# Both causal masks of a batch ahead of all its score products

## The chip, the cores and the metric

The kernel runs on one core of one Trainium2 chip. The metric is the device time of the whole program in microseconds (us), the median of the timed runs.

## The reference, cut to what matters

Sixteen batches of 112 tokens with 256 features first pass a cross attention with a context of 375 rows (only the start of the kernel). Then come four layers, each with a causal attention of 16 query heads over 4 key heads (64 wide, rotary positions) and a mixture of eight experts of which each token takes two:

```python
q = q * c + _rot_half(q) * sn
k = k * c + _rot_half(k) * sn
scores = jnp.einsum('bhqd,bhkd->bhqk', q, k) / sqrt(HD)
attn = jax.nn.softmax(scores + causal_bias, axis=-1)
out = jnp.einsum('bhqk,bhkd->bhqd', attn, v)
x = clip(res + out @ wo)          # then x = clip(res + moe(rms(x)))
```

## The kernel before

Each engine has its own instruction list, written by hand, and waits on semaphores. A layer's attention goes through the 16 batches one after another; I call one pass of `iteration(b)` **turn b**. Two batches (a pair, g = b // 2) share the projections: five blocks of heads, m = 0 (the keys) to 4 (the queries). TensorE computes a block (`heads_of`, L816), VectorE (DVE) turns it by the rotary tables (`rotate`: L1601, L1603, L1605, signal `d_rope`), and GpSimd (POOL) adds the two parts of blocks 1 to 4 (`add_rotated`, L591, signal `g_rope`). Pair g+1 is projected and rotated while pair g attends: block 0 and 1 in the even turn, blocks 2, 3, 4 in the odd turn, the last ones just before the next turn begins.

The 16 heads of a batch are two halves, p = 0 and p = 1. `scores(l, b, p)` writes one half into two banks of PSUM: p = 0 into banks 0 and 1, p = 1 into banks 2 and 3 (for b > 0). It first writes the causal mask with four small bf16 matmuls (L841), then adds the products of queries and keys (L846, 16 instructions in the trace), and signals `p_sc`. All run on two halves of 64 rows of the array at once. The same banks hold the projected blocks while they are rotated: in odd turns block 0 of the next pair (rotated in the turn before) lies in bank 1 and block 1 in bank 2; before an even turn, blocks 2, 3, 4 lie in banks 0, 1, 2. So the mask of a half may only be written when the rotation of what lay there is over: a wait on `d_rope`, by place. The products of half 0 need `g_rope` of block 2, those of half 1 that of block 4.

After the scores, DVE takes the maxima of each half (`maxima`, L1621, L1622), ScalarE (ACT) eight exponents of each half (L1273, an ACTIVATE and a read of the accumulator each, signal `a_exp`), DVE scales them (L1630, L1631). TensorE meanwhile projects the outputs of the batch before (`out_project`, L896). Behind that it starts the next block, which needs a bank of half 0 back, and therefore waits for the eight exponents of half 0: L816 in odd turns, L824 (the values) in even turns. Then come transposes of the probabilities (L861), more blocks, and the weighing (`weigh`, L872), with which a turn ends. In turns 10 to 13, DVE and POOL also rank the first nine batches' tokens and scatter them to memory (L623) for the experts; turn 15 (b = 15) waits for the first tile of these. Turn 0 of a layer has its scores computed in the layer before.

Of the kernel before, what the change touches and what calls it, by code (L numbers as in the profile page):

```python
# [13 lines left out]
B, S, D = 16, 112, 256  # L14
# [7 lines left out]
GN = GB * S  # L22
# [4 lines left out]
LOADS = 5  # L27
# [87 lines left out]
def xattn_ffn(nc, x, ctx_1024, w_sim, b_sim, W_qv, b_qv, ln1_w, ln2_w, wq, wk, wv, wo, wr, wg, wu, wd, const, out):  # L115
    with ExitStack() as stack:
        def sb(name, shape, dt=F32):
            return stack.enter_context(nc.sbuf_tensor(name, shape, dt))

        def sem(name):  # L120
            return stack.enter_context(nc.semaphore(name))
# [54 lines left out]
        qT = [q.rearrange("p (n t) -> p n t", n=8) for q in q_flat]  # L176
# [29 lines left out]
        rows_b = sb("rows_b", [128, 2, S], BF16)  # L206
        causal_b = sb("causal_b", [128, 2, S], BF16)
# [15 lines left out]
        def route_part(width):  # L223
# [35 lines left out]
        ps = stack.enter_context(nc.psum_tensor("ps", [128, 8, 512], F32))  # L259
# [29 lines left out]
        d_rope, d_max, d_norm, d_wo, d_lg, d_x, d_yr, d_oh, d_rt, d_pos, d_te, d_out, d_gate = (sem(n) for n in (  # L289
            "d_rope", "d_max", "d_norm", "d_wo", "d_lg", "d_x", "d_yr", "d_oh", "d_rt", "d_pos", "d_te", "d_out", "d_gate"))  # L290
# [17 lines left out]
        def bc(ap, axis, shape):  # L308
            return ap.unsqueeze(axis).to_broadcast(shape)
# [5 lines left out]
        def score_bank(b, p):  # L315

            return 2 * p if b else 2 - 2 * p
# [402 lines left out]
        def _(pe):  # L720
# [99 lines left out]
            def values(l, g, bank):  # L820

                for u in range(2):
                    for k in range(KD):
                        last = pe.matmul(ps[0:S, bank, u * D:u * D + NKV * HD], xnT[:, g % 2, k, u * S:u * S + S],  # L824
                                         wv_s[:, k, :], start=(k == 0), stop=(k == KD - 1))
                last.then_inc(p_v, 1)

            def scores(l, b, p):

                g, u = b // 2, b % 2  # L830
                if p == 0:
                    pe.wait_ge(d_rope, l * 40 + g * LOADS + 1)
                pe.wait_ge(g_rope, l * 32 + g * 4 + 2 * p + 2)

                def out(j):
                    return ps[0:S, score_bank(b, p) + j, 0:GN].rearrange("q (h k) -> q h k", h=4)

                for part, k0, k1 in ((0, 0, 64), (1, 64, S)):
                    for j in range(2):
                        js = slice(64 * j, 64 * j + 64)  # L840
                        pe.matmul(out(j)[:, :, k0:k1], causal_b[js, part, :], bc(rows_b[js, part, k0:k1], 1, [64, 4, k1 - k0]),  # L841
                                  start=(part == 0), stop=False)
                for i in range(4):
                    for j in range(2):
                        js = slice(64 * j, 64 * j + 64)
                        last = pe.matmul(out(j)[:, i, :], qT[g % 2][js, 4 * p + i, u * S:u * S + S],  # L846
                                         keys[g % 2][js, p, u * S:u * S + S], start=False, stop=(i == 3))
                last.then_inc(p_sc, 1)

            def layer(l, last_layer):  # L850

# [40 lines left out]
                def out_project(b, p):  # L892

                    pe.wait_ge(a_ot, l * 32 + 2 * b + p + 1)
                    for i in range(4):
                        last = pe.matmul(ps[0:S, 6, 0:D], oT[:, p, i * S:i * S + S], wo_s[:, 4 * p + i, :],  # L896
                                         start=(p == 0 and i == 0), stop=(p == 1 and i == 3))
                    if p:
                        last.then_inc(p_wo, 1)
# [60 lines left out]
                def expert_of(T):  # L960
                    return pe.value_load(tile_e[0:1, bass.ds(T, 1)], min_val=0, max_val=E - 1)
# [25 lines left out]
                def iteration(b):  # L987
                    g, odd = b // 2, b % 2
                    more = g + 1 < NP
                    if b:  # L990

                        if odd and more and b > 1:
                            pe.wait_ge(d_rope, l * 40 + (g + 1) * LOADS + 1)
                        if not odd:
                            pe.wait_ge(d_rope, l * 40 + g * LOADS + LOADS - 1)
                        if b == B - 1:
                            pe.wait_ge(m_xT, l * NT + 2)
                        scores(l, b, 0)
                        if b == B - 2:
                            out_project(b - 1, 0)  # L1000

                        if odd and more:
                            pe.wait_ge(d_rope, l * 40 + (g + 1) * LOADS + 2)
                        if b == RANK_STEP + 1:
                            pe.wait_ge(d_rt, l * NPART + 1)
                        if b == MID_STEP + 1:
                            pe.wait_ge(d_rt, l * NPART + 2)
                        scores(l, b, 1)
                        if b == 1:
                            pe.wait_ge(ld_wo, (l + 1) * 16 * 4)  # L1010
                        if b == B - 1:
                            pe.wait_ge(ld_mw, (l + 1) * 16 * 3 * E)
                            pe.wait_ge(d_te, l * 2 + 1)
                            e0, e1 = expert_of(0), expert_of(1)
                        if b != B - 2:
                            out_project(b - 1, 0)
                        out_project(b - 1, 1)

                    if b == 0:
                        pe.wait_ge(ld_wv, (l + 1) * 16)  # L1020
                        values(l, 0, 7)
                        pe.wait_ge(a_exp, l * 32 + 1)
                        pe.wait_ge(a_t1, l * B + 4)
                        heads_of(l, 1, 0, 2)
                    else:
                        pe.wait_ge(a_exp, l * 32 + 2 * b + 1)
                        if not odd:
                            values(l, g, 0)
                        elif more:
                            heads_of(l, g + 1, 2, 0)  # L1030
                        else:
                            up(0, 0, e0, wg_s, 0, m_g)
                    turn_probs(b, 0)
                    turn_probs(b, 1)
                    if b:
                        turn_x(b - 1)

                    if more:
                        if not odd:
                            pe.wait_ge(a_exp, l * 32 + 2 * b + 1)  # L1040
                            pe.wait_ge(a_t1, l * B + 2 * (g + 1) + 2)
                        heads_of(l, g + 1, 3 if odd else 0 if b else 1, 1 if b else 3)
                    elif odd:
                        up(0, 0, e0, wu_s, 1, m_u)
                    if b == MID_STEP:
                        pe.wait_ge(a_exp, l * 32 + 2 * b + 2)
                        count_rows(1, 3)
                    turn_probs(b, 2)
                    turn_probs(b, 3)
                    if b:  # L1050
                        route_logits(b - 1)

                    if more:
                        pe.wait_ge(a_exp, l * 32 + 2 * b + 2)
                        if b:
                            heads_of(l, g + 1, 4 if odd else 1, 2)
                    else:
                        pe.wait_ge(a_exp, l * 32 + 2 * b + 2)
                        if odd:
                            up(1, 1, e1, wg_s, 2, m_g)  # L1060
                    if b == RANK_STEP:
                        count_rows(0, 3)
                    if b == B - 2:
                        for T in range(2):
                            turn_tile(T, T, 1, 1, T * KD * SLOT)
                    if b == 0:
                        pe.wait_ge(moe_done, l + 1)
                    if not odd:
                        pe.wait_ge(a_v, l * NP + g + 1)
                    if odd and g + 2 < NP:  # L1070

                        pe.wait_ge(a_pt, l * 64 + b * 4 + 3)
                        for k in range(KD):
                            norm_turn(l, g + 2, k, 4, k * TN)
                    weigh(b)

                def tile(T, u, n, first=False, early=False, end=False, count=False):
# [23 lines left out]
                    if early and end:  # L1101
                        pe.wait_ge(m_h, l * NT + NT - 1)
                        scores(l + 1, 0, 0)
# [11 lines left out]
                for b in range(B):  # L1115
                    iteration(b)
# [971 lines left out]
```

## Time and profile before

| what | value |
|---|---|
| median of 3 runs | 1933.63 us (1933.07 to 1934.76) |
| profiled execution, from the first to the last instruction (span) | 1893.5 us |
| PE (TensorE matmul) busy | 1842.4 us, 97% |
| DVE / ACT / POOL busy | 1281.0 / 949.9 / 543.2 us |
| granted TensorE clock, mean | 0.994 |

The profile gives the span as the profiled execution's own time; the median of the runs lies 40.1 us above it, which is what lies before the first and behind the last instruction, and what no instruction of the kernel changes. PE's busy time is partly modelled, so 97% does not say that no wait matters. Below, PEld is TensorE's weight load and PE its matmul; each row of a timeline is start, duration, engine, line, operation, tiles and shapes, count, and in brackets the idle time just before it and what ended that.

### The profile page before, as it was taken

To read this page: it belongs to the slowest core of one execution; us is meant where nothing else is said; L and a number is where in the kernel's file an instruction comes from. 1 tells how busy PE (TensorE), PEld (TensorE's weight loads), DVE (VectorE), ACT (ScalarE), POOL (GpSimd) and SP (SyncE) were. 2 spreads that over 40 slices of the span, in tenths; PEclk is the share of its full clock that TensorE was granted. 3 is DMA by queue.
4 is the path that set the end of the run, shared out by engine and by line. 5 is a ranking of instruction groups with operands and counts; after the bars stand their busy time and mean duration, and the time that the engine had idled before them with its cause. 6 is when DMAs were issued, how large, how long until landed. Compare 5 with 4: busy or idle time off the path is not lost.

```text
span 1893.5 us, 36659 instructions
## 1 busy us (share of the span) xinstructions
PE 1842.4 (97%) x10612; PEld 1359.5 (72%) x10613; DVE 1281.0 (68%) x3173; ACT 949.9 (50%) x3625; POOL 543.2 (29%) x721
## 2 busy tenths in 40 slices
PE   7999999999999999999999999999999999999995
PEld 5887888766668888756667888766667888866663
DVE  4677778754467888764467888764466888855456
ACT  4647776622226777732225777642224777642221
POOL 4752113430022332540032332531031332520014
PEclk9999999999999999999999999999999999999998
DMA  6423220255653330245663340236663331136666
GB/s 165 130 71 107 101 101 6 85 139 143 154 149 102 116 115 7 85 122 142 145 157 89 118 130 27 85 94 147 145 164 93 128 116 44 43 92 149 147 163 172
DMA packets 255292, 212.37 MB, mean 112 GB/s; under 512 B 145826, under 2 KB 226420, under 8 KB 255028
## 3 DMA queue, kind: packets, MB, share of 16 engines
q1 hardware_dynamic: 240808, 174.74, 33.8%
q0 software_dynamic: 13952, 35.33, 6.3%
q8 instruction: 82, 1.34, 0.3%
q14 instruction: 70, 0.57, 0.1%
q10 hardware_dynamic: 380, 0.38, 0.1%
HBM read 137.32 MB, written 73.05 MB: 111 GB/s over the span
## 4 chain that ended last, share of the span: by engine, by line
PE 71%; DVE 9%; ACT 8%; issue 4%; POOL 4%; DMA 3%; SPq 1%; POOLq 0%; DVEq 0%; ACTq 0%
PE ps L930 24%; PE ps L956 12%; ACT parena L1273 8%; PE ps L816 7%; PE ps L896 6%; PE ps L872 4%; PE ps L846 3%; PE ps L861 3%; PE ps L824 3%; POOL qk L591 2%; DVE rope L1601 2%; PE ps L798 2%; PE ps L924 2%; DVE rmax L1621 2%; DVE rope L1605 2%
## 5 line engine op out<-in xcount | busy, mean ns | idle before, releaser
L930 PE MATMUL ps<-arena,xeT 128*128 x1120 | 509.5, 593 | 0.0
L1273 ACT ACTIVATE parena<-ps,nmax 112x112 f32<-112x112 f32 x1024 | 345.6, 387 | 95.3 <-DVE nmax L1622 95.3
L930 PEld LDWEIGHTS ps<-arena,xeT 128*128 128x128 f32 x1120 | 210.1, 190 | 193.5 <-issue 187.3
L591 POOL TENSOR_TENSOR qk<-qk,rope 128x448 f32<-128x448 f32 x128 | 146.3, 1143 | 548.9 <-DVE rope L1605 548.7
L1322 ACT ACTIVATE parena<-ps,er 128x512 f32<-128x512 f32 x140 | 96.2, 687 | 377.1 <-PE ps L930 377.1
L816 PE MATMUL ps<-xnT,wqk_s 128*128 128x224 f32 x1280 | 273.5, 357 | 0.0
L570 POOL DMA_INDIRECT y_in<-sorted_y,pos x114 | 111.2, 975 | 500.6 <-DMA sorted_y<-tarena 397.0
L1273 ACT ACTIVATION_READ_ACCUMULATOR parena<-ps,nmax 112x1 f32 x1024 | 245.9, 240 | 0.0
L896 PE MATMUL ps<-wo_s,oT 128*112 128x256 f32 x1024 | 237.9, 385 | 1.4 <-issue 1.4
L816 PEld LDWEIGHTS ps<-xnT,wqk_s 128*128 128x128 f32 x1280 | 233.5, 191 | 3.1
L1898 DVE SCALAR_TENSOR_TENSOR parena<-parena,ps 128x512 f32<-128x512 f32 x140 | 96.0, 686 | 181.5 <-ACT parena L1322 181.4
L896 PEld LDWEIGHTS ps<-wo_s,oT 128*112 128x112 f32 x1024 | 175.7, 177 | 43.1 <-issue 2.1
L623 POOL DMA_INDIRECT sorted_x<-x_sb,pos_x x128 | 126.8, 991 | 181.6 <-DVE pos_x L1825 147.9
L1621 DVE TENSOR_REDUCE rmax<-ps 112x8 f32<-112x896 f32 x128 | 139.0, 1086 | 56.9 <-PE ps L846 56.8
L1312 ACT ACTIVATE xeT<-ps,ln2T 128x128 f32<-128x128 f32 x280 | 87.4, 365 | 171.8 <-PE ps L924 167.7
L956 PE MATMUL ps<-arena,tarena 128*128 x640 | 153.2, 382 | 2.5 <-issue 1.8
L1282 ACT ACTIVATE tarena<-ps 112x448 f32<-112x448 f32 x256 | 130.2, 583 | 34.4 <-PE ps L861 33.8
L1631 DVE TENSOR_TENSOR parena<-parena,rrec 112x896 f32<-112x896 f32 x128 | 139.8, 1092 | 4.4
L1900 DVE SCALAR_TENSOR_TENSOR parena<-parena,er,ps 128x512 f32<-128x512 f32 x140 | 104.6, 747 | 54.6 <-PE ps L930 54.1
L1286 ACT ACTIVATE oT<-ps 128x448 f32<-128x448 f32 x128 | 69.5, 545 | 131.4 <-PE ps L872 131.4
L956 PEld LDWEIGHTS ps<-arena,tarena 128*128 128x128 f32 x640 | 119.1, 195 | 15.5 <-issue 4.5
L846 PE MATMUL ps<-qk 64*112 64x112 f32 x2048 | 123.4, 260 | 0.0
(207 smaller groups left out, 2785.2 us busy)
## 6 DMA issues: line engine op xcount, KB each, us to landing
sorted_y<-tarena SPq DMA_DIRECT2D x140, 128.0 KB
xe<-sorted_x SPq DMA_DIRECT2D x132, 130.0 KB, 2.5
arena<-in_L_ffn_wg_dram SPq DMA_DIRECT2D x32, 512.0 KB, 3.7
arena<-in_L_ffn_wu_dram SPq DMA_DIRECT2D x32, 512.0 KB, 4.6
arena<-in_L_ffn_wd_dram SPq DMA_DIRECT2D x32, 512.0 KB, 5.6
hid_d<-tarena SPq DMA_DIRECT2D x240, 64.0 KB
tarena<-hid_d SPq DMA_DIRECT2D x60, 256.0 KB, 2.8
hid_d<-parena SPq DMA_DIRECT2D x240, 64.0 KB
```

What stands on the lines that cost most here:

```text
L570: pool.indirect_dma_start(out=y_in[:, b % 2, k, :], out_offset=None, in_=sorted_y[0:FIRST * SLOT, :] if b < PARTS[0][1] else sorted_y, in_ ...
L591: pool.tensor_tensor(q, q, rope[m % 2][:, :], ALU.add).then_inc(g_rope, 1)
L623: pool.indirect_dma_start(out=sorted_x if h == 0 else sorted_x[0:HROWS - WHOLE * SLOT, :], out_offset=bass.IndirectOffsetOnAxis(ap=pos_x[: ...
L816: last = pe.matmul(ps[:, bank, x * TN:x * TN + TN], wqk_s[:, k, n, :], xnT[:, g % 2, k, :], start=(k == 0), stop=(k == KD - 1))
L846: last = pe.matmul(out(j)[:, i, :], qT[g % 2][js, 4 * p + i, u * S:u * S + S], keys[g % 2][js, p, u * S:u * S + S], start=False, stop=(i = ...
L896: last = pe.matmul(ps[0:S, 6, 0:D], oT[:, p, i * S:i * S + S], wo_s[:, 4 * p + i, :], start=(p == 0 and i == 0), stop=(p == 1 and i == 3))
L930: last = pe.matmul(ps[:, bank, :], xeT[u][:, k, :], w[:, bass.ds(e * 1024 + k * 512, 512)], start=(k == 0), stop=(k == KD - 1))
L956: last = pe.matmul(ps[:, 6, u * D:u * D + D], chunk, wd_s[:, bass.ds(e * 1024 + c * D, D)], start=(c == 0), stop=(c == 3))
L1273: last = act.activation(prob[:, n, :], ps[0:S, bank, h * S:h * S + S], ACT.Exp, bias=nmax[:, b % 2, n:n + 1], scale=SCALE, accum_out=rsum[ ...
L1282: act.activation(probT[:, unit, :], ps[0:S, 4 + unit % 2, 0:GN], ACT.Copy).then_inc(a_pt, 1)
L1621: step(dve.tensor_reduce(rmax[:, hs].rearrange("p (n h) -> p n h", n=2), heads(b, p), AX_X, ALU.max))
L1631: dve.tensor_tensor(prob[:, hs, :], prob[:, hs, :], bc(rrec[:, hs], 2, [S, 8, S]), ALU.mult).then_inc(d_norm, 1)
```

## The change

`scores` is cut into `causal` (the four mask matmuls) and `products` (the waits and the score products). In turns 1 to 13 and 15 the order is now: mask of half 0, mask of half 1, products of half 0, products of half 1. Turn 14 keeps its order, and so do the scores of turn 0. Since the mask of half 1 now stands ahead of the products that waited for `g_rope`, even turns get a wait of their own for the last rotation; the waits that protect banks 2 and 3 now stand ahead of both halves' products.

```diff
+            def causal(b, p):
+
+                for part, k0, k1 in ((0, 0, 64), (1, 64, S)):
+                    for j in range(2):
+                        js = slice(64 * j, 64 * j + 64)
+                        pe.matmul(score_out(b, p, j)[:, :, k0:k1], causal_b[js, part, :],
+                                  bc(rows_b[js, part, k0:k1], 1, [64, 4, k1 - k0]), start=(part == 0), stop=False)
+
+            def products(l, b, p):
 
                 g, u = b // 2, b % 2
                 if p == 0:
                     pe.wait_ge(d_rope, l * 40 + g * LOADS + 1)
                 pe.wait_ge(g_rope, l * 32 + g * 4 + 2 * p + 2)
...
-                        scores(l, b, 0)
+                        together = b != B - 2
+                        causal(b, 0)
+                        if not together:
+                            products(l, b, 0)
                         if b == B - 2:
                             out_project(b - 1, 0)
 
                         if odd and more:
                             pe.wait_ge(d_rope, l * 40 + (g + 1) * LOADS + 2)
+                        if not odd:
+                            pe.wait_ge(d_rope, l * 40 + g * LOADS + LOADS)
                         if b == RANK_STEP + 1:
                             pe.wait_ge(d_rt, l * NPART + 1)
                         if b == MID_STEP + 1:
                             pe.wait_ge(d_rt, l * NPART + 2)
-                        scores(l, b, 1)
+                        causal(b, 1)
+                        if together:
+                            products(l, b, 0)
+                        products(l, b, 1)
```

On TensorE, an odd turn's scores stood like this in the kernel before (L841 the masks, L846 the products, L896 the output projection; the names in brackets are the semaphores waited for):

```order
L841 MATMUL ps<-rows_b,causal_b 112x4x64 [waits g_rope,d_rope]
L841 MATMUL ps<-rows_b,causal_b 112x4x64
L841 MATMUL ps<-rows_b,causal_b 112x4x48 x2
L846 MATMUL ps<-qk 112x112 x8
L841 MATMUL ps<-rows_b,causal_b 112x4x64 [waits g_rope,d_rope]
L841 MATMUL ps<-rows_b,causal_b 112x4x64
L841 MATMUL ps<-rows_b,causal_b 112x4x48 x2
L846 MATMUL ps<-qk 112x112 x8
L896 MATMUL ps<-wo_s,oT 112x256 [waits a_ot]
```

The same place of the changed kernel, where L836 is the masks, L848 the products and L903 the output projection:

```order
L836 MATMUL ps<-rows_b,causal_b 112x4x64 [waits d_rope]
L836 MATMUL ps<-rows_b,causal_b 112x4x64
L836 MATMUL ps<-rows_b,causal_b 112x4x48 x2
L836 MATMUL ps<-rows_b,causal_b 112x4x64 [waits d_rope]
L836 MATMUL ps<-rows_b,causal_b 112x4x64
L836 MATMUL ps<-rows_b,causal_b 112x4x48 x2
L848 MATMUL ps<-qk 112x112 [waits g_rope,d_rope]
L848 MATMUL ps<-qk 112x112 x7
L848 MATMUL ps<-qk 112x112 [waits g_rope]
L848 MATMUL ps<-qk 112x112 x7
```

The second mask, with its wait for a rotation, moved from behind the first eight products to ahead of them. In an even turn the second mask waited for POOL's sum alone, and there the rows before were:

```order
L846 MATMUL ps<-qk 112x112 x8
L841 MATMUL ps<-rows_b,causal_b 112x4x64 [waits g_rope]
L841 MATMUL ps<-rows_b,causal_b 112x4x64
L841 MATMUL ps<-rows_b,causal_b 112x4x48 x2
L846 MATMUL ps<-qk 112x112 x8
L896 MATMUL ps<-wo_s,oT 112x256 [waits a_ot]
```

In the changed kernel even turns read as the odd turn above: POOL's sum is now waited for by the second eight products (L848), and the second mask waits for the rotation only. The lists of the other engines are the same in both kernels.

## Rows read from the trace of the kernel before

**Rows 1.** The page, part 1: busy time, share, instructions.

```profile
PE 1842.4 (97%) x10612; PEld 1359.5 (72%) x10613; DVE 1281.0 (68%) x3173; ACT 949.9 (50%) x3625; POOL 543.2 (29%) x721
```

**Rows 2.** The chain that ended last, turns 3 and 4 of layer 3: start, us, what.

```profile
1487.92 1.10 DVE rmax L1621
...
1489.25 5.50 ACT parena L1273 x32
...
1502.45 0.40 PE ps L841 x4
```

**Rows 3.** Timeline of turn 3 of layer 3.

```profile
1486.28 0.61 DVE L1605 TENSOR_TENSOR rope<-rope,cst 128x448 f32<-128x448 f32 x1
1486.60 0.18 PEld L841 LDWEIGHTS ps<-rows_b,causal_b 64*112 64x112 bf16 x4 [0.70 <-issue]
...
1486.84 0.96 PE L846 MATMUL ps<-qk 64*112 64x112 f32 x16
...
1487.63 0.35 PE L841 MATMUL ps<-rows_b,causal_b 64*112 64x256 bf16 x4
...
1487.83 0.96 PE L846 MATMUL ps<-qk 64*112 64x112 f32 x16
...
1492.11 1.49 PEld L816 LDWEIGHTS ps<-xnT,wqk_s 128*128 128x128 f32 x8
1492.26 1.68 PE L816 MATMUL ps<-xnT,wqk_s 128*128 128x224 f32 x8
```

**Rows 4.** Timeline of ScalarE, turn 3: end of the eighth exponent.

```profile
1491.81 0.24 ACT L1273 ACTIVATION_READ_ACCUMULATOR parena<-ps,nmax 112x1 f32 x1
```

**Rows 5.** Timeline of turn 4 of layer 3.

```profile
1500.48 0.69 DVE L1605 TENSOR_TENSOR rope<-rope,cst 128x448 f32<-128x448 f32 x1
...
1501.20 0.40 PE L841 MATMUL ps<-rows_b,causal_b 64*112 64x256 bf16 x4
1501.26 1.14 POOL L591 TENSOR_TENSOR qk<-qk,rope 128x448 f32<-128x448 f32 x1 [0.56 <-DVE rope L1605]
...
1502.45 0.18 PEld L841 LDWEIGHTS ps<-rows_b,causal_b 64*112 64x112 bf16 x4 [0.23 <-POOL qk L591]
...
1502.61 0.86 PEld L846 LDWEIGHTS ps<-qk 64*112 64x112 f32 x16
1502.69 0.96 PE L846 MATMUL ps<-qk 64*112 64x112 f32 x16
...
1503.58 3.29 PEld L896 LDWEIGHTS ps<-wo_s,oT 128*112 128x112 f32 x16
...
1506.42 0.24 ACT L1273 ACTIVATION_READ_ACCUMULATOR parena<-ps,nmax 112x1 f32 x1
...
1506.91 1.69 PEld L824 LDWEIGHTS ps<-wv_s,xnT 128*112 128x112 f32 x8
1507.12 1.89 PE L824 MATMUL ps<-wv_s,xnT 128*112 128x256 f32 x8
```

**Rows 6.** Waits, whole span: engine, line, releaser, us in total, times, longest.

```profile
PEld ps L841 <- POOL qk L591: 5.8, 24, 0.6
```

**Rows 7.** Timeline of VectorE, turn 1 of layer 3.

```profile
1457.17 0.61 DVE L1605 TENSOR_TENSOR rope<-rope,cst 128x448 f32<-128x448 f32 x1
...
1458.62 1.09 DVE L1621 TENSOR_REDUCE rmax<-ps 112x8 f32<-112x896 f32 x1 [0.84 <-PE ps L846]
```

**Rows 8.** The chain, turns 12 to 15 of layer 3.

```profile
1621.89 1.10 DVE rmax L1621
...
1655.34 2.94 DMA sorted_x<-x_sb,pos_x
...
1662.47 3.00 PE ps L872 x8
```

**Rows 9.** The chain, end of turn 14 of layer 2.

```profile
1228.74 1.65 PE ps L872 x8
```

**Rows 10.** A stretch: us, PE, PEld, DVE, ACT, POOL busy, granted clock, DMA share, GB/s.

```profile
1661.00:1666.00 5.00, 4.26 (x18) 1.86 (x20) 0.28 (x2) 2.46 (x8) 0.00 (x0) 0.66 0.01 4
```

More of the change, by code:

```diff
@@ L826, in values, with score_out @@
                 last.then_inc(p_v, 1)
-            def scores(l, b, p):
+            def score_out(b, p, j):
+                return ps[0:S, score_bank(b, p) + j, 0:GN].rearrange("q (h k) -> q h k", h=4)
+            def causal(b, p):
[5 more added lines that the diff above has]
+            def products(l, b, p):
                 g, u = b // 2, b % 2
@@ L833, in scores @@
                 pe.wait_ge(g_rope, l * 32 + g * 4 + 2 * p + 2)
[L835 to L842, printed above, removed]
                 for i in range(4):
@@ L845, in scores @@
                         js = slice(64 * j, 64 * j + 64)
-                        last = pe.matmul(out(j)[:, i, :], qT[g % 2][js, 4 * p + i, u * S:u * S + S],
+                        last = pe.matmul(score_out(b, p, j)[:, i, :], qT[g % 2][js, 4 * p + i, u * S:u * S + S],
                                          keys[g % 2][js, p, u * S:u * S + S], start=False, stop=(i == 3))
                 last.then_inc(p_sc, 1)
+            def scores(l, b, p):
+                causal(b, p)
+                products(l, b, p)
             def layer(l, last_layer):
```

## The prediction

> **What bounds the kernel now.** I read the page first: TensorE is busy 97% of the span and no other engine more than 68% [rows 1]. That speaks for a kernel that only TensorE's work can shorten, and the change removes no TensorE work: the same four mask matmuls and sixteen product instructions of each half run, in another order. So the question is only which waits grow or shrink, and 97% is partly modelled. I then read the chain that ended last over an attention stage. The reader is to see that in the turns 3 and 4 it doesn't stay on TensorE: it goes from the products of half 0 to the maxima (1487.92), through the sixteen exponents without a break (1489.25, 5.50 us), through the rotations and the sums on POOL, and comes back to TensorE at the mask of half 1 of turn 4 (1502.45) [rows 2]. So the products of half 0 of an odd turn lie at the head of a chain, and the mask of half 1 of an even turn at its foot. The change makes the first later and takes the second off the foot. Third, the timelines, for how tight each joint is.
>
> **Odd turns: what is late.** All times in turn 3 are counted from its first mask load, 1486.60 [rows 3]. Before: products of half 0 at +0.24 (1486.84), second mask at +1.03 (1487.63), its products 0.20 behind (1487.83). After: the second mask would follow the first at once and push the products by its own 0.20, if nothing held it. But it must wait for the second rotation, which read bank 2: that is the DVE row 1486.28, 0.61 long, which ends at 1486.89, +0.29 [rows 3]. Before, this wait stood at +1.03 and cost nothing. From a release to TensorE's restart I take 0.06: POOL's sum ends at 1501.26 + 1.14 = 1502.40 and the waiting mask load starts at 1502.45, so 0.05 [rows 5], and I take 0.06 for DVE, as at L816 below. The second mask then starts at +0.35, and the products follow 0.24 behind a mask that starts on an empty array (1502.45 to 1502.69 [rows 5]): +0.59 instead of +0.24, so **0.35 late**. Queued behind the waiting mask on TensorE are all products, the projection L896 and the rest of the turn; the first who waits for them is DVE with the maxima, then ScalarE.
>
> **Odd turns: does it reach TensorE?** Behind the projection, L816 needs half 0's bank and waits for the eighth exponent. That ends at 1491.81 + 0.24 = 1492.05 [rows 4], the load L816 starts at 1492.11 [rows 3]: exactly the release time, no slack. Its matmul follows at 1492.26, where the projection's matmuls leave the array. With the exponents 0.35 late, the load starts 0.35 late; if the whole lead of 0.15 of load over matmul is needed, the matmul is 0.35 late too, if none of it is, 0.20. I take 0.35 for the part of L816 and keep 0.20 for the range. The second branch, maxima, exponents, rotations, POOL, carries 0.35 as well.
>
> **Even turns: what comes back.** In turn 4 (from 1501.20) the last rotation ends at 1500.48 + 0.69 = 1501.17 [rows 5]. It moves with the turn's start, so the new wait for it costs nothing; the second mask costs the products of half 0 its 0.20. POOL's sum ended at +1.20, and 24 times in the whole span the mask waited for it, 5.8 us in all, 0.24 each [rows 6]. Now only the products wait there, so the load time of the mask, 0.16 to 0.24 (1502.45 to 1502.69), leaves this joint, and the wait is filled with work. Then the eighth exponent again: it ends at 1506.42 + 0.24 = 1506.66, while the load L824 starts at 1506.91 [rows 5], 0.25 behind, that is 0.19 above the release time 0.06. The 0.20 by which half 0 is late just uses that up. But L824's matmul ran only at 1507.12; with the load at the same time and the array free earlier (the projection comes some 0.16 sooner), it can gain up to 0.05.
>
> **Per pair, two paths.** Over the exponents twice: +0.35 in the odd turn, -0.05 in the even: **+0.30**. Over POOL: +0.35 at the products, minus the 0.16 of the mask that no longer stands behind the sum: +0.19. The later path decides: 0.30. With the smaller 0.20 at L816 the first path gives no more than 0.15, and POOL's 0.19 is the floor; with nothing back in the even turn the ceiling is 0.35.
>
> **The sum.** Pairs of turns (3, 4), (5, 6), (7, 8), (9, 10) in four layers: 16 x 0.30 = 4.8. Turn 1 (with 2): in layer 3 the second rotation ends at 1457.17 + 0.61 = 1457.78 and the maxima start at 1458.62 [rows 7], 0.84 later; in turn 3 that distance is 1487.92 - 1486.89 = 1.03 [rows 2, 3]. So here the products would be 0.35 + 0.19 = 0.54 late in the layers that look like this, and 0.20, for the mask alone, at least. I take the 0.30 of the other pairs, 1.2 in four layers, and keep 4 x 0.54 = 2.2 for the range. Turn 11: before turn 12 the maxima start 0.02 to 0.03 behind DVE's own ranking work (1621.89 [rows 8]), so nothing comes back or is lost in turn 12, and what turn 11 loses goes through DVE: its second rotation comes before a copy of the ranks and is early, so 0.20 for the mask alone, 0.8 in four layers. Turn 13: 0.35, since the chain goes on from it over POOL's scatters and DMA (1655.34 [rows 8]) to the first tile, which turn 15 waits for; 1.4. Turn 14 isn't changed. Turn 15 starts behind the DMA and has no rotation to wait for; its exponents are 0.20 later, which I cost at 0 since TensorE there works through the expert's matmuls; if that cover is gone it is 0.8. The expert stage shifts as it is. Together 4.8 + 1.2 + 0.8 + 1.4 = **8.2 us**. The span would be 1893.5 + 8.2 = 1901.7, and with the 40.1 around it, the median 1933.6 + 8.2 = **1941.8 us**, +0.42%. About 0.2%, 3.9 us, is what a measurement of this kernel can tell from no change.
>
> **A page beside a row.** In turn 4 the load of the products (1502.61) starts 0.16 behind the mask's load that waited, and the products' matmul 0.24 behind [rows 5]; in turn 3, where nothing waited, matmul follows matmul by 0.20 [rows 3]. If weight loads could pass a waiting mask, the products would follow by 0.20 in the odd turns too. The Trainium skill, page "TensorE: Matmul & The Clock Gate", section "The mechanism", says that loads for other row groups are pulled ahead of matmuls in flight, while matmuls stay in strict order. By the row the sum is 8.2, by that rule 24 waits less 0.04 each, 7.2.
>
> **The rivals.** (1) *It goes faster*: the filled wait in front of the second mask wins and the later maxima don't matter. It gives back 0.24 in each of the 24 cases [rows 6], 5.8 us, so 1927.8. It decides if the exponents have more than 0.35 of slack in odd turns; against it stands the load L816 that starts 0.06 behind the eighth exponent. (2) *Same*: the new wait is shorter than I read, so that only the mask's 0.20 counts. Then the pair costs 0.20 - 0.16 = 0.04 over POOL; 20 pairs with turn 1 give 0.8, and turns 11 and 13 0.20 each, 1.6: together 2.4, 1936.0. It decides if the rotation's signal is up before +0.20; the profile has its end at +0.29, and four queued instructions ahead of the projection can't hide that. (3) *Loads run ahead*, above: +7.2, 1940.8. (4) *Slower still*: every pair pays 0.35 (+0.8), turn 15 pays (+0.8), and the clock falls once more often. In layer 3 the weighing before turn 15 took 3.00 us with a mean granted clock of 0.66 over 5 us, after TensorE had waited for the tile; in layer 2 the same x8 took 1.65 [rows 8 to 10]. So one fall from 2.4 to 1.2 GHz costs 1.35 us. Two more make 2.7; together 8.2 + 4.3 = 12.5, 1946.1.
>
> **How the numbers follow.** Forecast 0.63, (1) 0.06, (2) 0.17, (3) 0.05, (4) 0.09. Faster is (1), 0.06; same is (2), 0.17; slower the rest, 0.77. The forecast's own range goes from 16 x 0.19 instead of 0.30, one clock fall less (8.2 - 1.8 - 1.35 = 5.1) to the upper bounds of all pairs with one fall more (8.2 + 0.8 + 1.0 + 1.35 = 11.4). The range for 8 in 10 goes further down, to +1.9, to take in most of (2), and up to +11.9: 1935.5 to 1945.5. Outside lie (1), a part of (2) and half of (4).
>
> **What would show it.** Right: in odd turns 3 to 9 the second mask starts some 0.35 behind the first, the maxima 0.35 later counted from the turn's first load (1.67 instead of 1.32), and L816 the same 0.35 later; in even turns no row of a mask waits for POOL, and L824 stands where it stood, at 5.7 from the turn's start. A pair takes 29.5 instead of 29.2. Wrong: the odd turn keeps its length though its maxima are late (slack that I don't see), or a turn 12 or 15 in which the loss vanishes behind other work of DVE or behind the DMA; or the even turns gain more than 0.05, so that the pair stays at 29.2.

## The result: 13 us slower, where 8 were forecast

| | before | changed |
|---|---|---|
| median of six runs each | 1932.29 us (1924.81 to 1934.76) | 1945.24 us (1941.95 to 1948.39) |
| ratio | | 1.0072, 95% interval [1.0056, 1.0089] |
| profiled execution, its span | 1893.5 us | 1940.1 us (its time 1941.95) |

The distance is 1945.24 - 1932.29 = 12.95 us; 8.2 were forecast, and +1.9 to +11.9 was the range. The direction was right, the size was not. The median itself lies just inside 1935.5 to 1945.5, but only since the median of before came out 1.3 us lower in six runs than in three; that is luck. The two spans differ by 46.6 us and so can't be compared as they stand; what this is due to is shown below, by further profiles of both kernels.

The head of the changed kernel's page: span, and busy time of the engines.

```profile
span 1940.1 us, 36630 instructions
PE 1861.9 (96%) x10612; PEld 1364.4 (70%) x10613; DVE 1277.9 (66%) x3173; ACT 949.8 (49%) x3625; POOL 542.6 (28%) x721
```

The work is the same and the shares are [rows 1] within two points. The order shows only in the joints. The timeline of the changed kernel, TensorE's loads, one row of its matmuls, and DVE, turns 3 and 4 of layer 3 and the start of turn 5:

```profile
1519.73 0.18 PEld L836 LDWEIGHTS ps<-rows_b,causal_b 64*112 64x112 bf16 x4 [0.70 <-issue]
1520.08 0.18 PEld L836 LDWEIGHTS ps<-rows_b,causal_b 64*112 64x112 bf16 x4 [0.17 <-DVE rope L1620]
1520.23 1.65 PEld L848 LDWEIGHTS ps<-qk 64*112 64x112 f32 x32
1525.58 1.43 PEld L816 LDWEIGHTS ps<-xnT,wqk_s 128*128 128x128 f32 x8 [0.30 <-ACT parena L1288]
...
1534.62 0.37 PEld L836 LDWEIGHTS ps<-rows_b,causal_b 64*112 64x112 bf16 x8 [0.70 <-DVE rope L1620]
1534.97 1.78 PEld L848 LDWEIGHTS ps<-qk 64*112 64x112 f32 x32
1540.32 1.57 PEld L824 LDWEIGHTS ps<-wv_s,xnT 128*112 128x112 f32 x8 [0.17 <-ACT parena L1288]
1541.93 0.93 PEld L868 LDWEIGHTS ps<-cst,parena 112*112 112x112 f32 x8
...
1549.12 0.18 PEld L836 LDWEIGHTS ps<-rows_b,causal_b 64*112 64x112 bf16 x4 [0.70 <-issue]
...
1520.32 1.75 PE L848 MATMUL ps<-qk 64*112 64x112 f32 x32
...
1519.41 0.62 DVE L1620 TENSOR_TENSOR rope<-rope,cst 128x448 f32<-128x448 f32 x1
1521.40 1.09 DVE L1636 TENSOR_REDUCE rmax<-ps 112x8 f32<-112x896 f32 x1 [0.91 <-PE ps L848]
```

The joints of turn 3 are as forecast, within 0.01 us: the second mask waits for the rotation and starts at +0.35 (1520.08), the maxima at +1.67 (1521.40), L816 at +5.85 (1525.58); the turn takes 14.89 instead of 14.60. In turn 4 no mask waits for POOL any more [rows 5, 6], L824 stands at +5.70, and the turn takes 1549.12 - 1534.62 = 14.50. Before it took 1515.82 - 1501.20 = 14.62 by the same loads, which the timeline of the kernel before has so:

```profile
1508.64 0.93 PEld L861 LDWEIGHTS ps<-cst,parena 112*112 112x112 f32 x8
...
1515.82 0.18 PEld L841 LDWEIGHTS ps<-rows_b,causal_b 64*112 64x112 bf16 x4 [0.70 <-issue]
```

The transposes L861 stood at 1508.64 - 1501.20 = 7.44 there; now (as L868) they stand at 7.31. So the even turn gains 0.13, though L824 is where it was.

### The profile page after: what moved, and what is told of

The parts are those of the page before. It is cut to its first block, busy times and chain, and to the rows that moved or that the text cites. A ratio compares the mean times of both kernels' runs of the same rounds, so it can differ in the third digit from the quotient of the medians.

```text
span 1940.1 us, 36630 instructions
## 1 busy us (share of the span) xinstructions
PE 1861.9 (96%) x10612; PEld 1364.4 (70%) x10613; DVE 1277.9 (66%) x3173; ACT 949.8 (49%) x3625; POOL 542.6 (28%) x721
## 4 chain that ended last, share of the span: by engine, by line
PE 83%; DVE 6%; ACT 4%; issue 3%; DMA 1%; another core or an unknown queue 1%; POOL 1%; SPq 0%; POOLq 0%; DVEq 0%; ACTq 0%
PE ps L937 23%; PE ps L963 12%; PE ps L816 11%; PE ps L903 9%; PE ps L879 5%; PE ps L848 5%; PE ps L868 4%; ACT parena L1288 4%; PE ps L824 2%; PE ps L798 2%; PE ps L836 2%; PE ps L931 2%; PE ps L742 1%; PE ps L780 1%
## 5 line engine op out<-in xcount | busy, mean ns | idle before, releaser
L816 PE MATMUL ps<-xnT,wqk_s 128*128 128x224 f32 x1280 | 281.1, 363 | 0.0
L570 POOL DMA_INDIRECT y_in<-sorted_y,pos x114 | 109.9, 964 | 501.0 <-DMA sorted_y<-tarena 396.1
L816 PEld LDWEIGHTS ps<-xnT,wqk_s 128*128 128x128 f32 x1280 | 235.4, 194 | 9.4 <-ACT parena L1288 7.8
L903 PE MATMUL ps<-wo_s,oT 128*112 128x256 f32 x1024 | 237.9, 385 | 1.5 <-issue 1.5
L903 PEld LDWEIGHTS ps<-wo_s,oT 128*112 128x112 f32 x1024 | 175.7, 177 | 43.2 <-issue 2.2
L623 POOL DMA_INDIRECT sorted_x<-x_sb,pos_x x128 | 126.2, 986 | 199.9 <-DVE pos_x L1840 166.2
L1301 ACT ACTIVATE oT<-ps 128x448 f32<-128x448 f32 x128 | 69.4, 545 | 137.8 <-PE ps L879 137.7
L868 PE MATMUL ps<-cst,parena 112*112 112x112 f32 x1024 | 122.7, 263 | 12.9 <-DVE parena L1646 9.4
```

The costliest lines, as they stand in the source:

```text
L570: pool.indirect_dma_start(out=y_in[:, b % 2, k, :], out_offset=None, in_=sorted_y[0:FIRST * SLOT, :] if b < PARTS[0][1] else sorted_y, in_ ...
L623: pool.indirect_dma_start(out=sorted_x if h == 0 else sorted_x[0:HROWS - WHOLE * SLOT, :], out_offset=bass.IndirectOffsetOnAxis(ap=pos_x[: ...
L816: last = pe.matmul(ps[:, bank, x * TN:x * TN + TN], wqk_s[:, k, n, :], xnT[:, g % 2, k, :], start=(k == 0), stop=(k == KD - 1))
L868: last = pe.transpose(ps[0:S, 4 + j, i * S:i * S + S], prob[:, p * 8 + j * 4 + i, :], ident[0:S, 0:S])
```

## Where the time lies, stretch by stretch

From here on all profiles of this study are used. The stretches are cut at the first mask load of a turn, as read above, and summed over the four layers (us):

| profile | turns 1 to 11 | 11 to 13 | turn 13 | turn 14 |
|---|---|---|---|---|
| before, first profile | 589.0 | 121.3 | 56.6 | 59.8 |
| before, second and third | 589.0, 589.1 | 121.3, 121.3 | 73.3, 67.6 | 73.7, 73.7 |
| changed, four profiles | 592.5, four times | 122.5, 122.3, 122.3, 122.3 | 79.4, 68.5, 75.2, 73.7 | 69.4, 74.2, 72.4, 72.4 |

Two things are to be seen. Up to turn 13 an execution of either kernel repeats to 0.2 us, and the order costs 3.5 + 1.1 = 4.6 us. Turns 13 and 14 do not repeat at all, and the first profile of before is the odd one out: each of its turns 13 took 14.15 us, in the others up to 21. The span that the prediction started from was that of an unusual execution. Of the 42.9 us between it and the second profile of before, 30.6 lie in turns 13 and 14. The rest of the span (the start, turns 0 and 15, the experts) takes 1066.8 us in it, 1079.1 and 1084.6 in the other two, and 1076.3 to 1078.9 with the new order: it varies by as much as the order costs up to turn 13, and the new order doesn't lengthen it. The mean granted clock was 0.994 in the first profile, 0.984 in the other two of before and 0.987 to 0.988 in the four changed ones.

## Experiments

Each time below is followed by its ratio to the kernel before, timed on the same chip, with the 95% interval in brackets.

**The two kernels again, unchanged.** A second profile of each, on one chip, the same as that of the first `split` and of `even_only` below.

> The kernel before, unchanged, for a second profile and more times. The first profile of before spans 1893.5 us, while the profile of the changed kernel spans 1940.1; there the time from the first score load of turn 13 to that of turn 15 is 35.2, 39.8, 35.8 and 38.0 us in the four layers against 28.0, 29.7, 28.1 and 30.5, and DVE, ScalarE and TensorE each stop for 2 to 4 us in turns 13 and 14 with no releaser among the engines. Theory 1 (the stops belong to every usual execution and the first profile of before was taken in an unusual one): the second profile of before spans 1920 to 1935 and has most of these stops, with turn 13 to 15 at 33 us or more. Theory 2 (the new order causes the stops): it spans about 1894 again, with no stop above 1 us in turn 13. Ratio 1.000 by both.

> The changed kernel, unchanged, for a second profile. Both theories: ratio about 1.005 to 1.008. Theory 1 allows that the stops in turns 13 and 14 change in size from one execution to the next; theory 2 wants the same stops, 32 us in all over the first profile of before. The turns 3 to 10 must repeat in any case: maxima 1.67 behind the first load in odd turns, 1.52 in even ones, a pair 29.39 us.

Measured: 1930.50 us, 1.0007 [0.9986, 1.0028], span 1936.4; and 1934.31 us, 1.0010 [0.9991, 1.0029], span 1933.9. Profiled time and span lie 1.9 us apart here as in all later runs (1938.27 and 1936.4), so the 40.1 us "around the span" are not what lies around it: the first profile is of a short execution, some 23 us shorter than the shortest timed run of before (1918.81). The changed kernel was nearly as fast as before on this chip, which no other run of it shows; what was different there is told at turn 13.

**Half 0 ahead of the wait.** In even turns the products of half 0 stand before POOL's wait again, but the mask of half 1 stays ahead of it.

```
-                        together = b != B - 2
+                        together = False
```

> No turn holds the products of half 0 back; in even turns the mask of half 1 is written after the products of half 0, before the wait for POOL's sum. If the chain over POOL's sum binds even turns, each of 24 of them gives back the mask's 0.16: 3.8 us less than before, ratio 0.998, and the pair takes 29.07 us instead of 29.23. If the exponents bind instead, 29.23 stays and the ratio is 1.000. By the theory that the order makes the stops in turns 13 and 14, they are those of before here, since turn 13 has the old order.

> The version that by the rows beats both: turns 1 to 11 took 585.8 us instead of 589.0. A second set of times and a second profile: 585.8 again, and a ratio to before of 0.998, with noise of 0.002.

Measured: 1928.61 us, 0.9992 [0.9971, 1.0014], and on another chip 1928.47 us, 0.9976 [0.9954, 0.9998]. Turns 1 to 11 take 585.8 and 586.0 us, 3.2 and 3.0 less than before. Turn 4 of layer 3 in the timeline of the first:

```profile
1524.89 0.18 PEld L836 LDWEIGHTS ps<-rows_b,causal_b 64*112 64x112 bf16 x4 [0.70 <-DVE rope L1620]
1525.04 0.86 PEld L848 LDWEIGHTS ps<-qk 64*112 64x112 f32 x16
1525.83 0.23 PEld L836 LDWEIGHTS ps<-rows_b,causal_b 64*112 64x112 bf16 x4
1526.14 0.86 PEld L848 LDWEIGHTS ps<-qk 64*112 64x112 f32 x16
1527.11 3.29 PEld L903 LDWEIGHTS ps<-wo_s,oT 128*112 128x112 f32 x16
1530.44 1.69 PEld L824 LDWEIGHTS ps<-wv_s,xnT 128*112 128x112 f32 x8
1539.35 0.18 PEld L836 LDWEIGHTS ps<-rows_b,causal_b 64*112 64x112 bf16 x4 [0.70 <-issue]
```

The mask is off the foot of POOL's chain and nothing is late at its head: L824 at +5.55 without a wait, the turn 14.46. This is the useful half of the change, 16 + 4 even turns x 0.16 = 3.2 us.

**Even turns alone, odd turns alone.** The new order only in even turns; then only in odd turns, with POOL's wait of the even ones back in its place.

```
+                        together = not odd and b != B - 2      (even_only)
+                        together = bool(odd)                   (odd_clean)
```

> The masks stand together in the even turns only. In the profile of the changed kernel an even turn took 14.49 us instead of 14.62 and an odd one 14.90 instead of 14.60. If that is the order of each by itself, a pair takes 29.10 us here, 0.13 under before, 24 x 0.13 = 3.1 us in all, ratio 0.998. If the late maxima of the even turns reach the next odd turn, the gain is gone and a pair stays at 29.23.

> The masks stand together in the odd turns only; even turns as in the kernel before, with the mask of half 1 behind POOL's sum. Turns 1 to 11 took 589.0 us (four layers together) in both profiles of the kernel before and 592.5 in both of the changed one. If the late maxima of an odd turn travel over exponents, rotations and POOL's sum and nothing gives time back in the even turn, each of the 20 pairs costs its whole 0.35: turns 1 to 11 take 596.0 us and a pair 29.58. If the even turns' gain of 0.13 and an odd turn's loss of 0.29 simply add, it is 589.0 + 20 x 0.29 = 594.8, a pair 29.52. If only the mask's own 0.20 counts, 593.0. The median, with its noise from turns 13 to 15, 1.002 to 1.005 of before.

Measured: even 1927.49 us, 0.9988 [0.9967, 1.0009], turns 1 to 11 586.3 us (-2.7). Odd 1952.29 us, 1.0106 [1.0082, 1.013], turns 1 to 11 595.3 us (+6.3), 11 to 13 122.4 (+1.1). The odd turns carry the whole loss. But 7.4 us up to turn 13 don't explain the 20.35 us of distance: the first sign that turn 13, an odd one, costs on its own. (The changed kernel timed beside it was 13.3 us over before. Of the 7.1 us between the two, turns 1 to 11 explain 2.8; the rest is not explained.)

**The mask twice.** The old order, but in odd turns 1 to 13 the mask of half 0 is written twice (so the scores carry it twice): the products are late by work, not by a wait.

```
+                        if odd and b < B - 1:
+                            causal(b, 0, False)
```

> The order of the kernel before, but in the odd turns 1 to 13 the mask of half 0 is added a second time ahead of its products (masked scores get twice the large negative number, which the softmax doesn't show). No wait moves. The products of half 0 are about 0.20 late by work alone. If lateness at the head of the chain is what costs, turns 1 to 11 take 589.0 + 20 x 0.20 = 593.0 us, or up to 0.06 less per pair where a load's lead hides it (591.8). If what costs is the wait in the queue and not the late products, TensorE's own time is 0.20 longer but the pair, which has a wait of 0.26 in it, stays at 29.23: 589.0.

> The changed kernel, a third set of times and a third profile, since the first two sets gave ratios of 1.0072 and 1.0010. By the rows, turns 1 to 13 cost 4.7 us and nothing else differs systematically: ratio 1.0024 over many runs, here between 1.000 and 1.005. If the turns 13 to 15 are systematically worse by the new order, the ratio is 1.005 to 1.008 again and the stretch from turn 13 to 15 takes over 148 us in the four layers, against 147.0 in the second profile of before.

Measured: 1941.23 us, 1.0046 [1.0027, 1.0064], turns 1 to 11 +3.85 us; the changed kernel beside it 1945.22 us, 1.0060 [1.0040, 1.0080]. In turns 1 to 11 lateness of the products costs whatever makes it. The distance to before is 9.3 us, of which turns 1 to 13 show 4.6; the other 4.7 are not explained.

**Early turns or late turns.** The new order up to turn 11, or from turn 12 on (with POOL's wait back ahead of the second mask in the even turns before that), and the two kernels beside them.

```
+                        together = b <= RANK_STEP + 1                    (until11)
+                        together = b > RANK_STEP + 1 and b != B - 2      (late_only)
```

> The new order only up to turn 11; from turn 12 on the products of half 0 stand ahead of the mask of half 1 again (in turn 12 still ahead of the wait for POOL, as in the kernel split). Theory A (the whole effect of the order lies in the length of turns 1 to 13, turns 13 to 15 are as long and as restless in any order): turns 1 to 11 take 592.5 us as in the changed kernel (before: 589.0), turns 11 to 13 121.3 to 122.0, and the ratio to before is 1.002 to 1.003, +3.5 to +5 us. Rival B (the late second mask of turns 12, 13 and 15 stretches the stops in turns 13 to 15, which is why 1.006 to 1.007 was timed): the same 592.5, and still a ratio of no more than 1.002, well below the changed kernel on the same chip.

> The mirror of it: the old order up to turn 11, the new one in turns 12, 13 and 15 alone. Theory A: turns 1 to 11 take 589.0 us as before, turns 11 to 13 about 121.5 to 122.4, so +0 to +1.5 us, a ratio within 1.001 of before. Rival B: turns 1 to 11 as before, and yet a ratio of 1.003 to 1.005 (+6 to +9 us), all of it in turns 13 to 15.

> The changed kernel once more, on the same chip as the two halves of it. Theory A: turns 1 to 11 592.5 us, turns 11 to 13 122.3 us, ratio 1.002 to 1.007, and over that of until11 by no more than 1.3 us of turns 11 to 13. Rival B: the ratio is the sum of the excesses of until11 and of late_only, with more than half from late_only.

> The kernel before, unchanged, profiled a third time, to see what of its time repeats: turns 1 to 11 589.0 us, turns 11 to 13 121.3 us to 0.1 us; turns 13 to 15 anywhere from 116 us (first profile) to 150 us (second), with waits for TensorE's or ScalarE's signals of 1 to 4 us in them if the first profile was the exception. Ratio 1.000 within its interval of 0.002.

Measured: until11 1929.86 us, 0.9993 [0.9971, 1.0014], though its turns 1 to 11 take 592.5 us; late_only 1942.39 us, **1.0061** [1.0038, 1.0083], its turns 1 to 13 as long as before; changed 1945.51 us, 1.0073 [1.0049, 1.0098]; before 1929.52 us, 0.9986 [0.9968, 1.0005]. Theory A, with which I had gone into these runs, falls: three turns a layer (12, 13, 15) hold most of the loss.

**One turn at a time.** The new order in turn 12, 13 or 15 alone, and the changed kernel without turn 13 (`together = b != B - 2 and b != 13`).

> The new order in turn 12 alone, which stands ahead of turn 13 and shifts the second rotation of turn 13 against it. Theory B12: ratio 1.002 or more. Theories B13 and B15: 1.000 within 0.002.

> The new order in turn 13 alone; all other turns as in the kernel before. Theory B13 (turn 13, whose exponents come 0.35 us later and whose turn is followed by POOL's scatters, is what costs): ratio 1.004 to 1.006, +8 to +12 us. Rivals: B15 (turn 15) or B12 (turn 12) give 1.000 here, within 0.002. The profiled turns 1 to 13 are as long as before (589.0 and 121.3 us) in every case.

> The new order in turn 15 alone. Theory B15 (the products of half 0 stand behind the wait for the second part of the ranks, and the first tile's exponents 0.20 us later push the experts' start): ratio 1.003 or more. Theories B13 and B12: 1.000 to 1.0005, since the profiled turn 15 shows DVE's maxima 0.20 us later and nothing more, 0.8 us in four layers at most.

> The changed kernel with turn 13 alone put back to the old order. Theory B13: the ratio falls from 1.006 to 1.007 to 1.000 to 1.002, that is what the new order up to turn 11 gave (0.9993) and at most the 0.8 us of turn 15. B15: it stays at 1.005 or more. B12: it stays at 1.003 or more.

| new order in | us | ratio |
|---|---|---|
| turn 12 | 1929.43 | 0.9992 [0.9975, 1.0008] |
| turn 13 | 1943.56 | **1.0059** [1.0040, 1.0079] |
| turn 15 | 1934.09 | 1.0019 [1.0006, 1.0032] |
| all but 13 (and 14) | 1930.94 | **1.0005** [0.9988, 1.0022] |

Turn 13 it is. The next rows show how. In the first profile of before, timeline of TensorE and DVE, end of turn 12 and start of turn 13, layer 1:

```profile
762.77 1.76 PE L816 MATMUL ps<-xnT,wqk_s 128*128 128x224 f32 x8
764.69 0.01 DVE L1601 LOAD_MASK_SELECT rope<-ps  x1
...
765.79 0.62 DVE L1605 TENSOR_TENSOR rope<-rope,cst 128x448 f32<-128x448 f32 x1
...
766.12 0.18 PEld L841 LDWEIGHTS ps<-rows_b,causal_b 64*112 64x112 bf16 x4 [0.70 <-issue]
766.27 0.86 PEld L846 LDWEIGHTS ps<-qk 64*112 64x112 f32 x16
```

The projection ends at 762.77 + 1.76 = 764.53, its second rotation starts 0.16 later and ends at +0.29 of turn 13, as in every odd turn. The same place in the third profile of before:

```profile
777.93 1.76 PE L816 MATMUL ps<-xnT,wqk_s 128*128 128x224 f32 x8
781.21 0.01 DVE L1601 LOAD_MASK_SELECT rope<-ps  x1 [1.30 <-PE ps L816]
...
781.27 0.18 PEld L841 LDWEIGHTS ps<-rows_b,causal_b 64*112 64x112 bf16 x4 [0.70 <-issue]
781.43 0.86 PEld L846 LDWEIGHTS ps<-qk 64*112 64x112 f32 x16
...
782.98 0.18 PEld L841 LDWEIGHTS ps<-rows_b,causal_b 64*112 64x112 bf16 x4 [0.69 <-DVE rope L1605]
```

Here DVE starts 1.52 behind the projection's end: the signal, by which TensorE tells DVE that the block is there, was late (the trace has its arrival 1.4 us behind the last matmul). The mask of half 1 waits for the rotation till +1.71. But the products of half 0 stand ahead of it and start at +0.16 all the same. And the same place with the new order in turn 13 (only13; its last row is ScalarE's, later in the turn):

```profile
777.54 1.76 PE L816 MATMUL ps<-xnT,wqk_s 128*128 128x224 f32 x8
780.81 0.01 DVE L1619 LOAD_MASK_SELECT rope<-ps  x1 [1.28 <-PE ps L816]
...
780.88 0.18 PEld L836 LDWEIGHTS ps<-rows_b,causal_b 64*112 64x112 bf16 x4 [0.70 <-issue]
782.57 0.18 PEld L836 LDWEIGHTS ps<-rows_b,causal_b 64*112 64x112 bf16 x4 [1.51 <-DVE rope L1623]
782.73 1.65 PEld L848 LDWEIGHTS ps<-qk 64*112 64x112 f32 x32
...
794.34 0.98 ACT L1300 ACTIVATE tarena<-ps 112x448 f32<-112x448 f32 x2 [3.64 <-remote]
```

The signal is as late, but now all products are queued behind the waiting mask: +1.85 instead of +0.16. Over the seven profiles with the new order in turn 13 (28 turns 13), the products of half 0 start at +0.50 to +1.85, 1.15 in the mean; over nine with the old (36, the first profile of before left out) at +0.16 in every one. The turn takes 18.86 in the mean against 17.06, and at least 17.00, where 19 of the 36 stay under 17. Four layers x 1.80 = **7.2 us**. Turn 14 adds 4 x (18.06 - 17.68) = 1.5.

"<-remote" in the last row is a second stop of the same kind: TensorE's transposes for ScalarE are long done, and the wait of 3.64 us ends when a batch of TensorE's signals arrives at once.

The rotation's signal was not late everywhere. In the second profile of the changed kernel, layer 1, it came in time, and the products start at +0.51:

```profile
777.23 1.76 PE L816 MATMUL ps<-xnT,wqk_s 128*128 128x224 f32 x8
779.15 0.01 DVE L1616 LOAD_MASK_SELECT rope<-ps  x1
...
780.57 0.18 PEld L836 LDWEIGHTS ps<-rows_b,causal_b 64*112 64x112 bf16 x4 [0.70 <-issue]
780.92 0.18 PEld L836 LDWEIGHTS ps<-rows_b,causal_b 64*112 64x112 bf16 x4 [0.17 <-issue]
781.08 1.65 PEld L848 LDWEIGHTS ps<-qk 64*112 64x112 f32 x32
```

Sorted by it, the same 64 turns 13 read (mean us of the turn, number of turns):

| rotation starts behind the projection's end by | old order | new order |
|---|---|---|
| 0.16 (in time) | 18.31 (12) | 17.13 (7) |
| 0.78 to 1.55 (late) | 16.43 (24) | 19.44 (21) |

So the new order costs 3.0 us a turn where the signal is late, and nothing that can be seen where it is in time. In layer 3 alone the late turns are 14.5 to 14.6 us in the old order and 17.8 to 19.3 in the new. On the chip of `base_again`, `after_again`, `split` and `even_only` it was in time in all sixteen turns 13, and there the changed kernel's ratio was 1.0010; on the two chips of the later profiles up to `skip13` it was late in 45 of 48, and on the one of them where the changed kernel ran its ratio was 1.0060 and 1.0073. Late products alone don't make 3.0 us, since the late signal puts them at +1.36 in the mean instead of +0.16, which is 1.2 us. The rest falls in the second stop; why that one is longer behind late products was not found.

**Without the scatters.** While this happens POOL issues fourteen scatters (L623) in turns 12 and 13. They are moved behind the last addition of turn 13, in the old and in the new order.

```
-                            if b == RANK_STEP + 2:
-                                scatter_first(l, 0, SOONER[0])
...
-                scatter_first(l, SOONER[1] + 1, PARTS[0][1])
+                scatter_first(l, 0, PARTS[0][1])
```

> The old order; the fourteen scatters that POOL issues among its additions in turns 12 and 13 are all issued behind the last addition of turn 13 instead. Theory S (the late signals of TensorE in turn 13 come with those scatters): turn 13 takes 14.2 to 14.6 us in all four layers, without a wait for a signal of over 1 us; turn 14 may still have one, since scatters now run there; the whole is slower than before if fourteen scatters of 1.25 us each show (up to 4 x 17 us), or the same if their cover holds. Rival R (the late signals have nothing to do with the scatters): turn 13 takes 15.4 to 21 us in most layers, as in the kernel before.

> The new order with the same fourteen scatters moved behind turn 13's additions. Theory S: turn 13 takes 14.5 to 15.0 us in all four layers instead of 17 to 21, and the time is 4 to 7 us (0.2 to 0.35%) over the kernel before with its scatters moved in the same way. Rival R: turn 13 still takes over 17 us, and the distance stays at 11 to 14 us (0.6 to 0.7%).

Measured: 1977.98 us, 1.0238 [1.0222, 1.0253], and 1984.35 us, 1.0280 [1.0262, 1.0297]. Loads of masks in turn 13, layer 1, and the first of turn 14, by the timeline of the new order:

```profile
792.20 0.18 PEld L829 LDWEIGHTS ps<-rows_b,causal_b 64*112 64x112 bf16 x4 [0.70 <-issue]
792.54 0.18 PEld L829 LDWEIGHTS ps<-rows_b,causal_b 64*112 64x112 bf16 x4 [0.17 <-DVE rope L1613]
792.70 1.65 PEld L841 LDWEIGHTS ps<-qk 64*112 64x112 f32 x32
...
806.63 0.18 PEld L829 LDWEIGHTS ps<-rows_b,causal_b 64*112 64x112 bf16 x4 [0.70 <-issue]
```

And of the old order:

```profile
789.41 0.18 PEld L834 LDWEIGHTS ps<-rows_b,causal_b 64*112 64x112 bf16 x4 [0.70 <-issue]
...
803.57 0.18 PEld L834 LDWEIGHTS ps<-rows_b,causal_b 64*112 64x112 bf16 x4 [0.70 <-issue]
```

Turn 13 takes 14.43 and 14.16, and the same to 0.01 us in all four layers; the mask waits 0.17. The late signals are gone from it, in eight turns of eight. They went with the scatters: in turns 12 and 13 no signal of TensorE is over 0.3 us late in these two profiles, and in turn 14, where the scatters now run, 36 and 40 are, by up to 3.3 us. The kernels pay for it (turn 14 takes 33 us behind the scatters) and so are slower, but the price of the order is now 1984.35 - 1977.98 = 6.4 us, as theory S had it, not 13. With five runs each this is known to some 4 us; the profiles have 3.3 + 1.1 in turns 1 to 13 and 1.1 in turn 13 itself, 5.5 together. The scatters are needed for the late signals of turn 13; the first profile of before shows that they don't always bring them.

## Why the forecast missed, point by point

- **Odd turns: what is late; Does it reach TensorE?** Right in each number: mask +0.35, products 0.35 late, L816 0.35 late with no slack. Of the 0.35 the turn lost 0.30.
- **Even turns: what comes back.** The place was right (L824 unmoved), the size wrong: 0.13 came back where I had allowed 0.05. I watched the load L824 and its matmul; the loads behind it, L868, came 0.13 sooner.
- **Per pair, 0.30.** Measured, as the mean over the 16 pairs: +0.31 - 0.13 = +0.18. So 16 x 0.18 = 2.9 instead of 4.8. Turn 1 (with 2): +0.15 a layer, 0.6 instead of 1.2. Together the 3.5 of the table. **Turn 11**: +0.28, 1.1 instead of 0.8 (turn 12 unchanged to 0.02, as said).
- **Turn 13: 0.35, 1.4 in all.** This is the step that failed. The 0.35 took it that the second rotation ends at +0.29 in turn 13 as in turn 3, and was read from the one profile in which no signal of TensorE was late in these turns. In most others the rotation's signal is up to 1.4 us late there, the new order puts all products behind it, and the turn grows by 3.0 us. Timed by itself (only13), the order of turn 13 costs 0.59%, 11.4 us (7.7 to 15.2), instead of 1.4. By the profiles, with the turns in which the signal was in time, the term is 7.2 (with turn 14, 8.7). That excess of 7.3 over the 1.4, less what the early turns and turn 11 cost below the forecast (6.8 - 4.6 = 2.2), gives 8.2 + 7.3 - 2.2 = 13.3, against 12.95 measured. That these two agree so closely is luck: the mean mixes chips, and the 4.6 of the early turns isn't seen in the times (below).
- **Turn 15, 0.** With the order there alone the ratio is 1.0019, 3.7 us, more than the 0.8 that I gave it without its cover; yet all turns but 13 give 1.0005. Not settled.
- **The median from the span plus 40.1.** Wrong, as shown; it did no harm to the distance, but a span 40 us off the timed runs should have been a question and not a term: the profile was of another kind of execution.
- **Rivals.** (1) is refuted by L816 at +5.85, (3) by the products' matmul at 1520.32 in turn 3, +0.59 and not less; (2), at 0.04 a pair, lies below the measured +0.18, which is about midway between it and my 0.30. The measured distance is near that of (4), 12.5, but not by its parts: the pair pays 0.18 and not 0.35, the mean granted clock is 0.987 in the seven profiles with the new order in turn 13 and in the nine with the old, and turn 15 is the one that stays open. None of the rivals named a rotation that comes late itself.

One thing stays open in the sum: turns 1 to 11 cost 3.5 us in the profile of until11, but its ratio is 0.9993 (interval to 1.0014, that is +2.7 us). Its turns 13 and 14 took 131.8 us in the profile, those of before 147.0 and 141.3; skip13 is alike, with 4.3 us up to turn 13 and 126.9 in turns 13 and 14, and a ratio of 1.0005; whether an early loss is regularly given back there, the runs can't tell.

## What to carry to other kernels

Don't put work that heads a chain behind a wait that only other work needs, even where the trace shows that wait to be short: in one turn of fifteen it mostly wasn't, and that turn cost more than the others together. Work without a consumer (here the mask) can be moved ahead of a wait; work with one stays ahead of it, as in the order of split, whose turns 1 to 11 are the shortest of those tried; its time, 0.9992 and 0.9976 of before, is hardly told from no change. And profile a kernel twice, on two chips if there are two, before its joints are used as terms: what repeats to 0.2 us can be read as a term, what doesn't needs its own run.

## What the runs showed of the hardware

TensorE's signals can be held. In turns 13 and 14, with POOL's indirect scatters around, signals of finished matmuls reached DVE and ScalarE late, by 0.6 to over 4 us, and often in a row: in the second profile of the changed kernel, layer 1, that of the projection L816 of turn 13, ended at +7.64, and the three behind it arrived at +11.78, +11.84, +11.90 and +11.94. DVE's own signals took 0.01 us in the same stretch. It is not turn 13 alone: in layers 1 to 3 POOL issues two indirect gathers (L570) in an even turn, and behind them the signal of the second products came 0.3 to 1.1 us late in turns 2 to 8 of every profile but the first of before. That cost nothing, as DVE had other work then and turns 1 to 11 are as long with it (589.0) as without. In the first profile of before no signal of TensorE is late in any turn. The view of all waits names a few of these "remote", and puts the rest down to the producer, which had long been done (changed kernel, first profile: waiter, releaser, us in all, times, longest):

```profile
PEld ps L836 <- DVE rope L1620: 24.7, 48, 1.5
...
DVE rmax L1636 <- remote: 12.0, 4, 3.5
```

The longest wait of the mask for the rotation is 1.5; in until11, with turn 13 in the old order, the same row ends with 0.7. The Trainium skill, page "Perfetto Trace Analysis", section "Tensor Engine Instruction (MATMUL, LD_WEIGHTS)", says that a matmul's end in the profile is estimated and that its semaphore update is pushed and propagated after that; the trace agrees, with 0.01 to 0.03 us between the two in undisturbed turns, and shows that it can be 4. What holds the signals was not found: in layer 3 the queues carry no weights at that time, only the scatters, and the signals are late there too.
